# Order of the four edge-table loads and place of the diagonal default, in a graph-transformer layer on one core

## What is computed

```python
w = jax.nn.softplus(edge_type_weights)
mask = jnp.full((N, N), -jnp.inf, dtype=dtype)
mask = mask.at[src, dst].set(w[edge_type - 1])        # a later edge overwrites an earlier one
diag = jnp.diagonal(mask)
mask = mask.at[idx, idx].set(jnp.where(jnp.isneginf(diag), w[3], diag))
scores = jnp.einsum('hnd,hmd->hnm', q2, k2) * scale + mask[None]
attn = jax.nn.softmax(scores, axis=-1)
```

## Time and profile before

| what | value |
|---|---|
| median of 3 runs | 503.61 us |
| the three runs | 503.61, 492.89, 503.67 us |
| the profiled execution | 478.61 us, of which the span shown is 476.8 us |
| mean granted TensorE clock over the span | 0.993 |
| PE busy | 466.1 us (98%) |
| DVE, ACT, POOL busy | 346.6, 258.5, 156.0 us |

### The profile page before, as it was taken

The page is one execution under the profiler, slowest core; times in us unless marked ns, Lnnn a source line. Parts: engine busy times, 40 slices in busy tenths (PEclk is TensorE's granted clock), DMA queues, the critical chain, the costliest instruction groups (busy, mean ns, idle before and its releaser), DMA issues.

```text
span 476.8 us, 7326 instructions
## 1 busy us (share of the span) xinstructions
PE 466.1 (98%) x2521; PEld 432.9 (91%) x2521; DVE 346.6 (73%) x796; ACT 258.5 (54%) x423; POOL 156.0 (33%) x176
## 2 busy tenths in 40 slices
PE   7999999999999999799999999999999999999996
PEld 5999999999999888699999999999998888888885
DVE  6968976677626237778889897898876994587394
ACT  3734533333324344668888788888875362163170
POOL 3136767767767762000210103022026000040200
PEclk9999999999999999799999999999999999999999
DMA  7876776566554446376676667577669854210463
GB/s 249 314 212 222 232 216 167 177 182 177 156 148 151 132 126 250 131 226 202 207 257 191 221 197 217 202 228 253 188 224 346 297 184 164 88 35 11 138 261 132
DMA packets 39049, 91.92 MB, mean 193 GB/s; under 512 B 7410, under 2 KB 20306, under 8 KB 38884
## 3 DMA queue, kind: packets, MB, share of 16 engines
q1 hardware_dynamic: 33604, 83.15, 54.2%
q0 software_dynamic: 4832, 7.45, 4.7%
q10 hardware_dynamic: 576, 0.85, 0.6%
HBM read 77.96 MB, written 13.47 MB: 192 GB/s over the span
## 4 chain that ended last, share of the span: by engine, by line
PE 57%; DMA 20%; issue 10%; POOL 7%; DVE 4%; POOLq 0%; ACT 0%; DVEq 0%; SPq 0%
PE PS L1331 21%; PE PS L1321 18%; DMA table<-evalue,where 15%; PE PS L1326 9%; POOL table L470 7%; PE PS L1459 4%; PE PS L1447 3%; PE PS L1583 2%; DMA mask<-table 1%; DMA U<-x 1%; DMA raw<-weights 1%; DMA key_dram<-V 1%; DMA U<-key_dram 1%; PE PS L1587 1%; DVE mask L1020 1%
## 5 line engine op out<-in xcount | busy, mean ns | idle before, releaser
L927 DVE TENSOR_TENSOR w_lo<-raw,w_hi 128x1024 fp32r<-128x1024 f32 x86 | 105.0, 1232 | 44.1 <-ACT w_hi L554 43.7
L554 ACT ACTIVATE w_hi<-raw 128x1024 fp32r<-128x1024 f32 x87 | 90.9, 1054 | 72.4 <-PE PS L1331 47.0
L470 POOL DMA_INDIRECT table<-evalue,where x96 | 104.4, 1087 | 48.0 <-issue 24.4
L1321 PE MATMUL PS<-xT_hi,w_hi 128*128 128x384 f32 x320 | 63.3, 339 | 3.3 <-DVE smax L1092 3.3
L1321 PE MATMUL PS<-xT_lo,w_hi 128*128 128x384 f32 x320 | 63.1, 339 | 0.0
L1326 PE MATMUL PS<-xT_hi,w_lo 128*128 128x384 f32 x320 | 62.0, 334 | 0.0
L1321 PEld LDWEIGHTS PS<-xT_hi,w_hi 128*128 128x128 f32 x320 | 57.1, 191 | 3.6 <-DVE smax L1092 3.6
L1321 PEld LDWEIGHTS PS<-xT_lo,w_hi 128*128 128x128 f32 x320 | 57.2, 191 | 0.0
L1326 PEld LDWEIGHTS PS<-xT_hi,w_lo 128*128 128x128 f32 x320 | 56.3, 188 | 0.0
L1331 PE MATMUL PS<-w_hi,T_hi 128*128 128x512 f32 x144 | 40.1, 391 | 0.0
L1331 PE MATMUL PS<-w_hi,T_lo 128*128 128x512 f32 x144 | 39.8, 389 | 0.0
(11 more groups left out here) (247 smaller groups left out, 810.9 us busy)
## 6 DMA issues: line engine op xcount, KB each, us to landing
raw<-weights SPq DMA_DIRECT2D x84, 512.0 KB, 4.5
turn<-U SPq DMA_DIRECT2D x16, 576.0 KB, 4.2
U<-turn SPq DMA_DIRECT2D x64, 144.0 KB, 2.9
U<-key_dram SPq DMA_DIRECT2D x32, 192.0 KB, 4.2
mask<-weights SPq DMA_DIRECT2D x9, 512.0 KB, 4.8
table<-Q POOLq DMA_DIRECT2D x4, 576.0 KB, 10.7
V<-conv SPq DMA_DIRECT2D x4, 512.0 KB, 5.3
U<-table POOLq DMA_DIRECT2D x3, 576.0 KB, 7.8
```

Source lines behind the costliest of these rows:

```text
L470: pool.indirect_dma_start(tables[g], bass.IndirectOffsetOnAxis(ap=where[:, k:k + 1], axis=0), evalue[:, k:k + 1], None, bounds_check=N * N ...
L554: act.activation(w_hi[slot][:], raw[slot][:], ACT.Copy).then_inc(hi_ready[slot], 1)
L927: dve.tensor_tensor(w_lo[slot][:], raw[slot][:], w_hi[slot][:].bitcast(F32), ALU.subtract).then_inc(lo_ready[slot], 1)
L1321: pe.matmul(o, w_hi[slot][:, k * P:(k + 1) * P], src[part][:, k, :], start=(k == 0 and part == 0), stop=False)
```

## The change

`default_diagonal` and its tile `bare` go. In its place POOL writes `w[3]` to the 384 diagonal entries of table 0 in device memory before the first scatter, by a strided DMA whose source is one column of `ew`; the scatters into table 0 wait for it, and an edge on the diagonal overwrites it. `pool.wait_ge(prep, 7)` waits for DVE's L959, which finishes `ew`. POOL loads tables 1, 2, 3 first and table 0 last. DVE folds table 2 into `later[0]` where `default_diagonal` stood (after the split of r = 6), then, after the split of r = 7, folds table 3 into it, tests the result, and copies it over `mask` once that has come. The count of large DVE instructions for merging stays at three tests and three predicated copies.

```diff
--- before.py
+++ after.py
@@ -204,7 +204,6 @@
         row_bo = Q2[:].rearrange("p k n -> p (k n)")[:, 0:2 * D].rearrange("p (r d) -> p r d", r=2)
         k2f = U[:, NT * D:2 * NT * D]
         blank = Q2[:, 0:NT, :]
-        bare = U[:, 4608:4608 + NT * P].rearrange("p (t n) -> p t n", t=NT)
         bias_rows = k2f[BIAS_ROW:BIAS_ROW + 2, 0:D]
         raw_down = k2f[:, D:D + KB * R].rearrange("p (k r) -> p k r", k=KB)
         raw_up = k2f[:, D + 512:D + 512 + KB * R].rearrange("p (k r) -> p k r", k=KB)
@@ -261,7 +260,6 @@
         where_ready = sem("where_ready")
         blanked = sem("blanked")
         first_mask_in = sem("first_mask_in")
-        diag_step = sem("diag_step")
         scattered = [sem(f"scattered{g}") for g in range(STREAMS)]
         table_in = [sem(f"table_in{g}") for g in range(1, STREAMS)]
         mask_step = sem("mask_step")
@@ -462,17 +460,22 @@
             pool.wait_ge(key_calc, 1)
             pool.dma_start(key_dram, erow[:, 0:P]).then_inc(key_out, 16)
 
+            pool.wait_ge(prep, 7)
+            pool.wait_ge(scattered[0], 16)
+            pool.dma_start(tables[0][::N + 1, :].rearrange("(t p) o -> p (t o)", p=P),
+                           ew[:, 3:4].broadcast_to([P, NT]), allow_slow_non_contiguous=True).then_inc(scattered[0], 16)
+
             for k in range(CH):
 
                 g = QUARTERS[k % STREAMS]
                 pool.wait_ge(where_ready, k // CJ + 3)
-                pool.wait_ge(scattered[g], 16 * (k // STREAMS + 1))
+                pool.wait_ge(scattered[g], 16 * (k // STREAMS + 1 + (g == 0)))
                 pool.indirect_dma_start(
                     tables[g], bass.IndirectOffsetOnAxis(ap=where[:, k:k + 1], axis=0),
                     evalue[:, k:k + 1], None, bounds_check=N * N - 1,
                     oob_is_err=False).then_inc(scattered[g], 16)
-            for g, into in enumerate([mask[:]] + later):
-                pool.wait_ge(scattered[g], 16 * (DEEP + 1))
+            for g, into in [(1, later[0]), (2, later[1]), (3, later[2]), (0, mask[:])]:
+                pool.wait_ge(scattered[g], 16 * (DEEP + 1 + (g == 0)))
                 if g == 0:
 
                     pool.wait_ge(lo_ready[A_SLOTS[3]], FIRST // 4 + 1)
@@ -999,28 +1002,26 @@
                                              in1=dst[0][:, j, :].bitcast(F32), op0=ALU.add,
                                              op1=ALU.subtract).then_inc(bank_free[a % 4], 1)
 
-            def default_diagonal():
-
-                dve.wait_ge(first_mask_in, 16)
-                dve.wait_ge(id_in, 16)
-                for t in range(NT):
-                    dve.scalar_tensor_tensor(out=bare[:, t, :], in0=mask[:, t, t * P:(t + 1) * P], scalar=ABSENT,
-                                             in1=ident, op0=ALU.is_equal, op1=ALU.mult).then_inc(diag_step, 1)
-                dve.wait_ge(diag_step, NT)
-                for t in range(NT):
-                    dve.copy_predicated(mask[:, t, t * P:(t + 1) * P], bare[:, t, :].bitcast(U32),
-                                        ew[:, 3:4].broadcast_to([P, P])).then_inc(diag_step, 1)
-                dve.wait_ge(diag_step, 2 * NT)
-
-            def merge_table(g):
-
+            def fold_table(g):
+
+                dve.wait_ge(table_in[0], 16)
                 dve.wait_ge(table_in[g], 16)
                 dve.tensor_scalar(present, later[g], ABSENT, None, ALU.not_equal).then_inc(mask_step, 1)
-                dve.wait_ge(mask_step, 2 * g + 1)
+                dve.wait_ge(mask_step, 2 * g - 1)
+                dve.copy_predicated(later[0].rearrange("p t n -> p (t n)"),
+                                    present.bitcast(U32).rearrange("p t n -> p (t n)"),
+                                    later[g].rearrange("p t n -> p (t n)")).then_inc(mask_step, 1)
+                dve.wait_ge(mask_step, 2 * g)
+
+            def merge_tables():
+
+                dve.tensor_scalar(present, later[0], ABSENT, None, ALU.not_equal).then_inc(mask_step, 1)
+                dve.wait_ge(first_mask_in, 16)
+                dve.wait_ge(mask_step, 5)
                 dve.copy_predicated(mask[:].rearrange("p t n -> p (t n)"),
                                     present.bitcast(U32).rearrange("p t n -> p (t n)"),
-                                    later[g].rearrange("p t n -> p (t n)")).then_inc(mask_step, 1)
-                dve.wait_ge(mask_step, 2 * g + 2)
+                                    later[0].rearrange("p t n -> p (t n)")).then_inc(mask_step, 1)
+                dve.wait_ge(mask_step, 6)
 
             for a in range(FIRST):
                 job(a)
@@ -1056,9 +1057,9 @@
                 if r == K2_FIRST + 1:
                     k2_lo(0)
                 if r == 6:
-                    default_diagonal()
-            for g in range(STREAMS - 1):
-                merge_table(g)
+                    fold_table(1)
+            fold_table(2)
+            merge_tables()
 
             def pv_sum(j, h):
                 r = slice(64 * h, 64 * h + 64)
```

## The result

| | before | after |
|---|---|---|
| median | 494.11 us (20 runs, 490.04 to 503.67) | 494.81 us (20 runs, 490.16 to 500.14) |
| profiled execution | 478.61 us, span 476.8 | 494.17 us, span 492.4 |
| mean granted clock, profiled | 0.993 | 0.979 |

The ratio of after to before, formed from the undisturbed runs of each, is 1.0189, 95% interval 1.0113 to 1.0265; over all 20 runs the medians differ by 0.14%. Much of what follows comes from that.

A forecast was written before the change was run, and what follows sets the result against it. PE's jobs and the scatters-to-mask path were taken as nearly equal, the late mask costing 6.1 us. -3.6 (earlier `pv(0, 0)`) + 0.15 (early write) = -3.4 us, so 503.61 became 500.2 us; 8-in-10 range 489.5 to 505.

The forecast's parts named there:

- What bounds the kernel: PE's jobs and the scatters-to-mask path nearly equal; late mask costs PE 3.3 us idle and about 2.8 us of half clock.
- the last one of the sum: Whole kernel: the 3.4 us gain carried unchanged from the profiled execution to the timed runs, 503.61 to 500.2 us.
- slower scatters: POOL's scatters: if they took the timed runs' extra time, PE waits longer for the mask and the saving stays nearly the same.
- The early write: POOL's diagonal write before the scatters: hidden in idle time, landed before the fourth scatter at 34.70, costing +0.15 us.
- The rival of a late write: Diagonal write into table 0 lands late, delaying the fourth and all later scatters; 506.6 us at an 18 us landing; chance 0.08.
- The loads: Table loads behind the last scatters: table 2 lands at 180.3 instead of table 0 at 181.33, a gain of 1.0 us.
- the landings don't move: Rival at the table loads: table 2 lands at 182.2, only 0.6 us won, 503.2 us; chance 0.17.
- The diagonal's 1.47 us: On DVE ahead of the merges: making the diagonal, 1.47 us, is gone; the remaining work stays 9.12 us.
- The slow test: DVE merge test beside POOL's L504 took 1.42 us, others 0.76; might miss it, up to 0.66 us more, left out.
- The clock's share: PE's `rq` job: with only 0.7 us idle the clock stays full, saving about 2.8 us, of which some 1.7 becomes waiting.
- Queued behind the wait: On DVE, the split of r = 7 and the reads follow the table waits; PE needs that split only late in its job.
- nothing is to be seen: Rival for the whole time: runs of one kernel differ by 10.8 us; called no mechanism, sets the range; no chance of its own.

The follow-up runs named there:

- the second profile of before: The kernel before, unchanged, run again in a later job: 499.49 us (12 runs), ratio 1.0043 to the kernel before in the same job.
- the parts: Against the kernel before: new order of loads and folds without the early write, 499.69 us, ratio 0.9963; early write with the old order, 496.59 us, ratio 0.996.
- the mask late on purpose: Last 24 chunks scattered a second time in each kernel: before 503.86 us, after 501.56 us, new order alone 503.65 us, early write alone 501.63 us.
- the later profile: Profile of the kernel before with its last 24 chunks scattered a second time: median 503.86 us (5 runs).
- the early write alone: Kernel before plus the diagonal written in memory, old order of loads and merges; with the last 24 chunks scattered twice, 501.63 us (4 runs).
- the one of such a job with 48: The kernel before with only the first 48 of its 96 scatters: 489.62 us (10 runs), ratio 0.9872 to the kernel before.

## Why the prediction was wrong

- **What bounds the kernel.** Read rightly for the execution shown: PE waited for the mask, and the wait and the half clock after it cost up to 6 us. From the scores to the end, executions without the wait take 5.2 to 5.5 us less (285.9 and 285.7 against 291.1). But that execution was of a kind that the 20 runs beside it don't contain, and I took it as the kernel's usual course.
- **The step that failed** is the last one of the sum: "The three timed runs of before lie 14 to 25 us above that execution, and nothing in the profile shows where their time went. I carry the difference over unchanged." The difference lies in PE ahead of the scores (206.68 instead of 185.67 in the second profile of before). The last scatter is 7.1 us later there (179.78), but DVE comes to the diagonal only at 196.84 and finds table 0 landed, and the last read ends 1.4 us before `rq` starts. None of the seven profiles with slow stretches in kernels with all scatters has a wait of PE for the reads. The term of 3.4 us then becomes zero. I had named the one case in which this sum survives, slower scatters, and not the opposite one, slower PE, which the shown wait of only 3.3 us made the obvious danger: by that row some 4 us lost by PE before 185 us, with nothing else later, end it (an estimate).
- **The number** 500.2 us is off by 5.4 us from 494.81. The median of the three runs that I started from lay 9.5 us above that of the 20; of this the 3.4 us of forecast gain and the 0.7 us between the two kernels are to be taken off. The range held the time, but by its width: the mechanism that the number stood for was absent.
- **The direction.** Predicted 0.7% faster, measured 1.0189 at first, then 0.996 to 1.0043 for the parts and the kernel before itself, and 0.9969 (0.9936 to 1.0003) for the change. The first ratio has no cause in the change that any run shows: in the profile of after nothing that the change added or moved is waited for, and the stretches that hold its lost time are in before as well. Nor can it come from the 20 and 20 runs above: the longest run of after that the ratio takes in, 497.29 us, over the shortest run of before, 490.04 us, is 1.0148. It must count an execution of before that is not among the 20, and the only one on record beside them is the profiled one of 478.61 us; that it was counted is not shown. The 0.14% between the medians of the 20 is no difference.
- **The early write: right.** Issued at 24.07, 0.77 us, nothing waited for it; the fourth scatter at 34.33 (34.70 before). The first key job was not delayed, and PE waited for it 0.24 us instead of 0.70; over all profiles that wait is 0 to 2.04 us with the write and 0 to 1.40 us without, so the +0.15 us can't be seen. The rival of a late write fell. One working beside this term was wrong: the Trainium skill (DMA: Bandwidth & Descriptors, Bandwidth) gets its 10.5 ns from the 0.67 us and the 64 packets of a whole transfer, not from one engine's time, so it is not to be divided by 16 and doesn't bear out the 12 ns. Taken whole it would be 384 x 10.5 ns = 4.0 us (an estimate), still short of the fourth scatter. The sum didn't use it.
- **The loads: half wrong.** Their issues came as told, one after another behind the last scatter. That table 2 would be there 1.0 us before table 0 used to be did not show: with the mask late on purpose, DVE started 6.24 us after the last scatter was issued, against 5.93 in before. The rows had given 181.33 - 172.64 = 8.69 for before; that was one long wait and one long landing (2.74 us of waiting for the last scatter, where the later profile has 1.45, and 5.95 us from the load's issue to DVE's start, where that has 4.48), and the new order's 7.66 was measured against it. This is the rival "the landings don't move", in this one term.
- **The diagonal's 1.47 us: right.** 1.45 us between first step and last read (12.74 against 11.29), and by the profiles the early write alone gives the whole gain. The slow test, left out of the sum, was gone too: the three tests of after took 0.75 to 0.76 us.
- **The sum where the mask is waited for.** Predicted 2.5 us from the reads; 2.3 us by medians that overlap, 1.1 us by the profiles to the last read. What is missing is the landing of table 2: a loss of 0.3 us in place of a gain of 1.0. The clock's share could not show there, as PE waited for 26.8 us and 28.2 us.
- **Queued behind the wait.** I noted the split of r = 7 behind DVE's wait and called it harmless, since PE needs it late in `rk`. With a mask late by 30 us PE waited for it 19.8 us; the claim holds only for a short wait.
- **The rival "nothing is to be seen"** was set aside as noise and not a mechanism. It was the case, and it had a mechanism.

## What to carry to other kernels

When the profiled execution lies outside the runs beside it, first ask which engine lost the difference: time lost by the engine that waits is slack for the thing it waits for, and a saving can vanish in it altogether. A wait of 3 us at the meeting of two paths of 190 us is worth its price only in those executions in which it is there; a gain of this kind is to be looked for in the tail of long runs (here none of 12 above 475.5 us instead of five in 23 at 478, too few to be sure), not in the median. To measure the length of a hidden path, make it late on purpose: with 24 more scatters, the runs spread over 4 to 5 us instead of 15, and the steps behind the last scatter could be read from one profile each.

## What the runs showed of the hardware

- In some jobs PE issues weight loads and matmuls in small groups that start 0.7 us or a multiple of it apart, for 16 to 24 us and again, with all the scatters, for 3 to 15 us, with nothing that it waits for in the profile, and at half clock in part of it (0.62 over 20 us). This happened only while indirect scatters ran on POOL's software queue: in the profile of after of the first result, in all six profiles of kernels with 96 scatters of the two jobs where the kernel before had a median of 498 and 499 us, and in the one of such a job with 48; not in the first profile of before (478.61 us), and in none of the four profiles without scatters, one of which is of such a job. By these medians it costs about 25 us in 473. It is not bound to a chip: the chip on record as number 10 was free of it in one job and had it in another.
- The Trainium skill (DMA: Bandwidth & Descriptors, Queues, rings and completion order) tells of rings of descriptors and of a row of queues for the runtime's own transfers, refill among them. No run here shows that this is the way by which the scatters reach PE. Every profile, with slow stretches or without, counts 20 packets and 0.33 MB on the queue that it calls q8 instruction, so that traffic doesn't tell them apart.
- The strided write of 384 single elements took 0.77 us to issue, as much as a load of 576 KB (0.80 us), and had landed before the fourth scatter, 9.5 us after its issue had ended, was due: that one did not wait.
